# Attention of a transformer block in steps of 256 queries and four heads, with the softmax sums as products of their own

## The reference, cut to what matters

```
mod = silu(condition) @ Wada + bada            # six vectors a batch: shifts, scales, gates
xm  = layernorm(x, g1, be1) * (1 + sc_a) + sh_a
q, k, v = split(xm @ Wqkv)                     # 16 heads of 32
s   = (q @ k.T) * 32**-0.5, causal mask        # per batch and head, 1024 x 1024
x   = x + gt_a * ((softmax(s) @ v) @ Wproj + bproj)
xm  = layernorm(x, g2, be2) * (1 + sc_m) + sh_m
x   = x + gt_m * (gelu(xm @ W1 + b1) @ W2 + b2)
```

## Time and profile before

| | before |
|---|---|
| median of 3 runs | 3526.39 us |
| profiled execution | 3530.63 us |
| its span | 3528.9 us |
| mean granted TensorE clock | 0.981 |
| TensorE busy (products) | 3353.2 us, 95% |
| VectorE busy | 1776.7 us, 50% |
| ScalarE busy | 1199.3 us, 34% |
| GpSimd busy | 1025.6 us, 29% |

### The profile page before, as it was taken

One profiled execution on the slowest core, in us unless ns is written; L12 is line 12 of the kernel. 1 busy time (PEld: TensorE's weight loads), 2 busy tenths in 40 slices (PEclk: granted clock), 3 DMA queues, 4 the chain that ended last, 5 costly groups with the idle time before them and its releaser, 6 DMA issues.

```text
span 3528.9 us, 59322 instructions
## 1 busy us (share of the span) xinstructions
PE 3353.2 (95%) x19052; PEld 2422.8 (69%) x19052; DVE 1776.7 (50%) x2288; ACT 1199.3 (34%) x2578; POOL 1025.6 (29%) x1267
## 2 busy tenths in 40 slices
PE   7889999999999999998857999999999999999999
PEld 4645555555555555543327989998998998899898
DVE  4455665665666655655615444444444444444442
ACT  2135555455555455545531111111211111121111
POOL 3222232222222222222225323333332333333232
PEclk9989999999999999999988999999999999999999
DMA  5445555455555555554443222222122222212220
GB/s 205 157 135 163 161 160 173 149 166 159 164 156 166 166 154 161 161 165 142 130 107 93 71 59 65 57 56 71 51 67 60 65 57 56 71 51 71 56 60 13
DMA packets 227209, 392.77 MB, mean 111 GB/s; under 512 B 30160, under 2 KB 96720, under 8 KB 227080
## 3 DMA queue, kind: packets, MB, share of 16 engines
q1 hardware_dynamic: 213648, 369.42, 36.3%
q10 hardware_dynamic: 13440, 22.03, 1.8%
HBM read 271.71 MB, written 119.11 MB: 111 GB/s over the span
## 4 chain that ended last, share of the span: by engine, by line
PE 90%; DVE 4%; ACT 2%; issue 2%; DMA 1%; POOL 0%; SPq 0%; ACTq 0%; DVEq 0%; POOLq 0%
PE psH L740 21%; PE psY L753 20%; PE psA L652 15%; PE psA L595 10%; PE psT L629 8%; PE psP L719 5%; PE psA L591 5%; PE psS L609 4%; DVE mx L1043 2%; ACT e L822 2%; DVE psS L1039 1%; PE psP L729 1%; PE psT L555 1%; PE psA L629 1%; ACT xm_full L800 1%
## 5 line engine op out<-in xcount | busy, mean ns | idle before, releaser
L822 ACT ACTIVATE e<-psT 128x512 f32<-128x512 f32 (+3 forms) x1440 | 635.7, 491 | 671.0 <-PE psT L629 664.2
L1275 POOL TENSOR_TENSOR h_l<-h_full,h_h 128x256 fp32r<-128x256 f32 x512 | 488.6, 954 | 1122.1 <-DVE h_h L1201 1122.1
L1043 DVE TENSOR_REDUCE mx<-psS 128x4 f32<-128x2048 f32 (+3 forms) x384 | 666.4, 1757 | 211.1 <-PE psS L609 205.5
L922 ACT ACTIVATE h_full<-psH,b1c 128x256 f32<-128x256 f32 x512 | 244.0, 477 | 1333.1 <-PE psH L740 1333.1
L1201 DVE CAST h_h<-h_full 128x256 fp32r<-128x256 f32 x512 | 151.0, 295 | 899.5 <-ACT h_full L922 899.4
L740 PE MATMUL psH<-a_h,w1p_h 128*128 128x256 f32 x2048 | 578.3, 282 | 7.5 <-DVE a_l L1196 7.5
L652 PE MATMUL psA<-e,vst 128*33 128x512 f32 (+3 forms) x3072 | 578.2, 498 | 5.2 <-ACT o_sb L830 3.6
L740 PE MATMUL psH<-a_h,w1p_l 128*128 128x256 f32 x2048 | 580.7, 284 | 0.0
L740 PE MATMUL psH<-a_l,w1p_h 128*128 128x256 f32 x2048 | 580.3, 283 | 0.0
L1301 POOL TENSOR_SCALAR_AFFINE_SELECT e<-e 128x256 f32<-128x256 f32 x512 | 217.4, 426 | 927.6 <-ACT e L822 926.5
L629 PE MATMUL psT<-qst,kst 97*128 97x512 f32 (+3 forms) x1440 | 442.0, 377 | 31.7 <-ACT e L822 30.6
(11 more groups left out here) (101 smaller groups left out, 4035.5 us busy)
## 6 DMA issues: line engine op xcount, KB each, us to landing
qk_split<-qk_hl SPq DMA_DIRECT2D x128, 512.0 KB, 3.6
kst<-qk_split SPq DMA_DIRECT2D x128, 256.0 KB, 4.0
qst<-qk_split SPq DMA_DIRECT2D x128, 256.0 KB, 4.3
values<-vaug ACTq DMA_DIRECT2D x64, 264.0 KB, 2.1
vst<-values SPq DMA_DIRECT2D x32, 528.0 KB, 4.1
attended<-o_sb SPq DMA_DIRECT2D x256, 66.0 KB
xin<-in_x_dram SPq DMA_DIRECT2D x64, 256.0 KB, 4.8
kmx<-qk_split SPq DMA_DIRECT2D x32, 512.0 KB, 4.3
```

The lines of the kernel that those rows point to most:

```text
L822: act.activation(e[:, s % ERING, hd, 0:w], score_bank(s, hd, with_a)[:, 0:w], ACT.Exp, scale=SCALE)\
L922: act.activation(h_full[:, m % 4, :], psH[:, m % 4, 0:RA], ACT.Gelu, bias=b1c[:, m:m + 1])\
L1043: reduce = dve.tensor_reduce(mx[:, part, :, qt], psS[:, :, col:col + w], AX_X, ALU.max)
L1275: return pool.tensor_tensor(dst, full, high.bitcast(F32), ALU.subtract)
```

## The change

A step is now one chunk of keys by up to 256 queries for all four heads. The chunks run through quarters of the queries, the last quarter first; an item has 20 steps, a body 40, and two steps are a slot. A score bank holds two heads. Each head's values stand on output rows 32 x head, without the column of ones. The sums are separate products of `ones` (128 x 32) with exponentials, into the second half of `psO`: in the 4 slots of an item that hold the diagonal, with both chunks; in the other 6, with `es`, the sum of the slot's two tiles, which GpSimd adds. `psO` is copied after each quarter. q and k are loaded by quarters of the rows, for four heads in one transfer of 1 KB rows; the first quarter of k has two places. The sums come out 32 times over, one row of each head is stored to `s_dram`, and each MLP block loads them broadcast and inverts them on VectorE in four pieces, two blocks ahead; those of blocks 0 and 1 are inverted before the MLP starts. The normalised block goes back into `xin`, so its next load waits for the transposes. The step numbers of all other work are moved to fit 40 steps.

```diff
-NCH = 12
-IT_STEPS = 24
-BODY_STEPS = 48
+NCH = 20
+SLOTS = NCH // 2
+BODY_STEPS = 2 * NCH
+BODY_SLOTS = 2 * SLOTS
 ERING = 8
+SRING = 2
-A_SHARES = ((6, 0, 6), (2, 8, 2), (5, 1, 5, 1)) * 4
+A_SHARES = ((6, 0, 6), (2, 8, 2), (8, 4)) * 4
-TURN_AT = (40, 41, 42, 43)
-SPLIT_HI_AT, SPLIT_LO_AT = 44, 45
+TURN_AT = (34, 35, 36, 37)
+SPLIT_HI_AT, SPLIT_LO_AT = 38, 39
-LN_STATS_AT, LN_AGGR_AT, LN_NORM_AT = (20, 22, 24, 26), 28, (32, 34, 36, 38)
-MAX_AT = {1: (1, 3), 3: (1, 4), 5: (1, 5), 7: (1, 6), 9: (1, 7), 11: (1, 8)} | {15: (2, 0), 19: (2, 1), 23: (2, 2)}
+LN_STATS_AT, LN_AGGR_AT, LN_NORM_AT = (14, 16, 18, 20), 22, (26, 28, 30, 32)
+MAX_AT = {1: (1, 3), 3: (1, 4), 5: (1, 5), 7: (1, 6), 9: (1, 7), 11: (1, 8)} | {15: (2, 0), 17: (2, 1), 19: (2, 2)}
-O_COPY_AT = {6: (0, 0), 2: (1, 1)}
+O_COPY_AT = {10: (0, 0), 16: (0, 1), 0: (1, 2), 2: (1, 3)}
+LOAD_QK_AT = {8: 3, 14: 2, 18: 1}
+LOAD_K0_AT, LOAD_Q0_AT = 2, 0
+INVERT_AT = {5: 0, 9: 1, 14: 2, 15: 3}
...
+                b, hg = group(u, ahead)
+                src = src[:, :, :, bass.ds(b * T + QUART * p, QUART)]
+                sp.dma_start(tile[0:2 * HD, :, cols].bitcast(F32), src.rearrange("j c s r -> (c s) j r"))\
+                  .then_inc(done[p], 16)
...
+                bank = score_bank(s, hp, with_a)
+                for d in range(2):
+                    hd = 2 * hp + d
+                    mm = pe.matmul(bank[:, d, 0:w], kst[0:97, hd, key_cols(kt, h)], qst[0:97, q0 // HALF, hd, q0 % HALF:q0 % HALF + w],
+                                   start=True, stop=True, skip_group_check=True)
+                mm.then_inc(sem("scores_ready"), 1)
+
+            def added_sums(u, t):
+                h, i = divmod(t, SLOTS)
+                n = (u * 2 + h) * len(ADDED_SLOTS) + ADDED_SLOTS.index(i)
+                pe.wait_ge(sem("added"), n + 1)
+                past(pe, "pe")
+                for hd in range(GH):
+                    mm = pe.matmul(psO[HD * hd:HD * (hd + 1), QUART:2 * QUART], ones[:],
+                                   es[:, ADDED_SLOTS.index(i) % SRING, hd, :], start=False, stop=True,
+                                   skip_group_check=True)
+                mm.then_inc(sem("summed"), 1)
...
                 for d in range(2):
-                    half, kt, q0, w = CHUNKS[c + d]
-                    for hd in range(2):
-                        j = 2 * (pair % 2) + hd
-                        cols = slice(q0 - HALF * half, q0 - HALF * half + w)
-                        mm = pe.matmul(psO[64 * hd:64 * hd + VW, cols], vst[:, pair // 2, kt, VW * j:VW * (j + 1)],
-                                       e[:, (s + d) % ERING, hd, 0:w], start=(kt == 0), stop=True,
+                    quarter, kt, q0, w = CHUNKS[2 * i + d]
+                    c = q0 - QUART * quarter
+                    for hd in range(GH):
+                        mm = pe.matmul(psO[HD * hd:HD * (hd + 1), c:c + w], vst[:, h, kt, HD * hd:HD * (hd + 1)],
+                                       e[:, (2 * t + d) % ERING, hd, 0:w], start=(kt == 0), stop=True,
                                        skip_group_check=True)
-                    mm.then_inc(sem("pv_done"), 1)
+                if i in DIAG_SLOTS:
+                    for d in range(2):
+                        quarter, kt, q0, w = CHUNKS[2 * i + d]
+                        c = QUART + q0 - QUART * quarter
+                        for hd in range(GH):
+                            mm = pe.matmul(psO[HD * hd:HD * (hd + 1), c:c + w], ones[:],
+                                           e[:, (2 * t + d) % ERING, hd, 0:w], start=False, stop=True,
+                                           skip_group_check=True)
+                mm.then_inc(sem("pv_done"), 1)
...
                     if s % 2 == 1 and not (isinstance(u, int) and u == 0 and s == 1):
-                        values(u, s - 3)
+                        t = s // 2
+                        if t >= 2 and (t - 2) % SLOTS in ADDED_SLOTS:
+                            added_sums(u, t - 2)
+                        values(u, t - 1)
...
-            dve.wait_ge(sem("sums_loaded"), 16)
-            dve.reciprocal(x1[:, 1], x1[:, 0]).then_inc(sem("sums_inverted"), 1)
+            def invert(u, k):
+                dve.wait_ge(sem("o_loaded"), 5 * 16 * (u + 1))
+                dve.reciprocal(oin[:, 1, k], oin[:, 1, k]).then_inc(sem("sums_inverted"), 1)
...
+            for k in range(KT):
+                invert(0, k)
             for m in range(FT):
                 prepare_step(0, 0, m)
+                if m == BASE_AT:
+                    for k in range(KT):
+                        invert(1, k)
...
+            def add(u, t):
+                h, i = divmod(t, SLOTS)
+                if i in ADDED_SLOTS:
+                    n = ADDED_SLOTS.index(i)
+                    pool.wait_ge(sem("exp_done"), (u * BODY_STEPS + 2 * t + 2) * 2)
+                    wait(pool, sem("summed"), (u * 2 + h) * len(ADDED_SLOTS) + n - SRING + 1)
+                    past(pool, "pool")
+                    pool.tensor_tensor(es[:, n % SRING], e[:, 2 * t % ERING], e[:, (2 * t + 1) % ERING], ALU.add)\
+                        .then_inc(sem("added"), 1)
```

More of the change, by code:

```diff
@@ L77, in score_chunks @@
     out = []
[L78 to L81, removed]
+    for quarter in reversed(range(4)):
+        for kt in range(2 * quarter + 2):
+            q0 = max(QUART * quarter, P * kt)
+            out.append((quarter, kt, q0, QUART * (quarter + 1) - q0))
     return out
@@ L108 @@
 DIAG = [c for c, (_, kt, q0, _) in enumerate(CHUNKS) if q0 == P * kt]
-assert len(CHUNKS) == NCH
+DIAG_SLOTS = [i for i in range(SLOTS) if 2 * i in DIAG]
+ADDED_SLOTS = [i for i in range(SLOTS) if i not in DIAG_SLOTS]
+LAST_SLOT = {CHUNKS[2 * i][0]: i for i in DIAG_SLOTS}
+assert len(CHUNKS) == NCH and len(ADDED_SLOTS) % SRING == 0
 assert sorted((qt, part) for chunks, _ in MAXES for qt, part, _, _ in chunks) == \
@@ L261, in build @@
         mlp.close()
-        qk_loaded = [sem(f"qk_loaded{s}") for s in range(2)]
+        q_loaded = [sem(f"q_loaded{p}") for p in range(4)]
+        k_loaded = [sem(f"k_loaded{p}") for p in range(4)]
         m_loaded = [sem(f"m_loaded{s}") for s in range(2)]
@@ L315, in load_x @@
                 if r == 0:
-                    wait(sp, sem("xn_ready"), ia)
+                    if isinstance(ia, int) and ia <= AHEAD + 1:
+                        wait(sp, sem("xn_ready"), ia)
+                    else:
+                        sp.wait_ge(sem("a_formed"), (ia - 1) * A_N + A_TURNS)
                     past(sp, "sp")
@@ L411, in _ @@
             load_max(0, 0)
-            load_qk(0, 0)
+            load_k(0, 0, 0)
+            load_q(0, 0, 3)
+            for p in (1, 2, 3):
+                load_k(0, 0, p)
+            for p in (2, 1):
+                load_q(0, 0, p)
             load_max(0, 1)
@@ new lines, in values @@
+            def values(u, t):
+                if t < 0:
+                    u, t = u - 1, t + BODY_SLOTS
+                h, i = divmod(t, SLOTS)
+                it = u * 2 + h
+                if i == 0:
+                    pe.wait_ge(v_loaded[h], (u + 1) * 16)
+                if CHUNKS[2 * i][1] == 0:
+                    wait(pe, sem("o_copied"), it * 4 + 3 - CHUNKS[2 * i][0])
+                if i in DIAG_SLOTS:
+                    pe.wait_ge(sem("masked"), it * len(DIAG) + 2 * DIAG_SLOTS.index(i) + 2)
@@ L659, in body @@
                 for s in range(BODY_STEPS):
-                    h, r = divmod(s, IT_STEPS)
-                    for hd in range(2):
-                        scores(u, s, hd, with_a)
+                    h, r = divmod(s, NCH)
+                    for hp in range(2):
+                        scores(u, s, hp, with_a)
                     if with_ln and s in TURN_AT:
@@ L854, in body @@
                 for s in range(BODY_STEPS):
[L855 to L856 removed]
+                    h, r = divmod(s, NCH)
                     exps(u, s, with_a)
[L858 to L861 removed]
+                    if r in O_COPY_AT:
+                        back, n = O_COPY_AT[r]
+                        if not (isinstance(u, int) and u == 0 and h < back):
+                            o_copy(u, h - back, n)
                     if with_a and item_ended(s - 1) is not None and item_ended(s - 1) < A_NV:
@@ L1048, in max_join @@
                 dve.wait_ge(sem("max_reduced"), i * NMX + NMX)
-                dve.tensor_tensor(mxc[:], mx[:, 0], mx[:, 1], ALU.max).then_inc(sem("max_joined"), 1)
+                first, second = (mx[:, part].rearrange("p h (s t) -> p s h t", s=2) for part in range(2))
+                dve.tensor_tensor(mxc[:], first, second, ALU.max).then_inc(sem("max_joined"), 1)
             def max_row(u, ahead):
@@ L1313, in body @@
                     mask(u, s)
+                    if s % 2 == 1:
+                        add(u, s // 2)
                     if with_ln and s == SPLIT_LO_AT:
```

277 lines of the change are left out of this document (130 added, 147 removed).

## The result

| | before | after |
|---|---|---|
| median of 8 runs | 3528.89 us | 3542.51 us |
| lowest, highest | 3525.66, 3532.33 us | 3538.59, 3551.08 us |
| profiled execution, its span | 3530.63, 3528.9 us | 3540.59, 3538.9 us |
| mean granted TensorE clock | 0.981 | 0.967 |

The ratio is 1.0043 [1.0032, 1.0055]: the changed kernel is 0.4% slower. The forecast was 1.4% faster. The number lies inside the range and the sign is wrong.

What follows compares the result with a forecast made beforehand. TensorE's stream was taken to bound 13 of 16 bodies. From 3530.6 us, terms of -73, +43, -27, -5 and +12 made -50, so 3480.6 us, or 3476 us for the timed median; range 3405 to 3560 us.

Steps and rivals of the forecast that it cites:

- the clock's term: At the new body ends, falls of TensorE's granted clock to half were set at 1 us a body, 12 us.
- the change of stage: Between attention and MLP: 12 us off ahead of the first product, 6 back before the residual; 5 us gained (0 to 12).
- Values and sums: TensorE's attention products: four heads on four column tiles take 14.2 us an item, 2.8 less, -73 us over 13 bodies.
- The rival with 1.5 us an item: Short 128-column passes on four tiles can't start within 0.05 us of each other: 48 us more, 3524 us; chance 0.08.
- GpSimd's adds: Six adds an item on GpSimd, at 3 us each, come in time for TensorE and cost nothing.
- The end of a body: TensorE waits 3.6 us for xm_l behind a third VectorE reduction, once in each of 12 bodies: 43 us lost.
- The clock rival: The clock falls at each body end, costing 82 us instead of 12: 3546 us, slower; chance 0.17.
- The last three bodies: Attention without projection: 38.5 us an item, a gain of 4.5 in each of 6 items, 27 us (0 to 40).
- The MLP: Each block gains 4 x 1.64 us of VectorE work, with hidden tiles cast three steps ahead: no change in time.
- The rival without a body-end wait and at full clock: No wait comes up at the body end and the clock stays: -43 and -12, 3421 us; chance 0.20.

Runs made afterwards that it cites:

- kernel with both edits: The changed kernel with TensorE's two loops over bodies written out and the transposes, split and normalising two steps earlier: 3456.04 us, 0.9792 of before.

## Why the prediction was wrong, by its steps

The step that failed by most is the clock's term: 12 us were set down, and the runs put it near 40. Behind it stands a term that the sum lacks, the return of TensorE's loop, 37 us of holes in the middle bodies. With the stream's gain 10 us too good and the change of stage of the wrong sign, the span became 10 us longer where 50 us less were forecast.

The distances and starts of the two traces divide the 10.0 us by which the span grew: start +1.7, bodies with projection +29.1, last bodies -23.5, change of stage +3.4, MLP -0.7. The forecast had -3 for the first (one item), -15 for the second (25 items at -2.8, +43, +12), -27, -5 and nothing. The second is where it failed. There the terms as measured are about -59 for the products, +39.5 for holes and `xm_l`, +9 for other short waits (30.9 us before, 40.2 after) and some +40 for the clock, which makes +30.

- **Values and sums: right, a little too good.** The kernel with both edits has few other losses, so it is the best place to read this: its bodies with projection take 48.2 us less than before over 25 items. The clock cost 10 us of that (below), and other short waits are equal within 1 us, so the products are worth about 59 us where 25 x 2.8 = 70 was forecast, 2.4 us an item. Eight passes of 256 columns take 0.45 us (408.56 to 409.01), four every 0.22, for 0.21 forecast. The rule of the Trainium skill (TensorE: Matmul & The Clock Gate, Part 3), that four row tiles give 3.07x and three column tiles 2.38x, would have made the item dearer than before by an estimated 1.1 us; the stream of four column tiles here shows no such loss.
- **Can TensorE be fed: yes.** In the group of 16 passes from 409.01 us the last eight, of 128 columns, take 0.22 us, 0.027 us each, and the four of a set start 0.007 us after one another. The rival with 1.5 us an item (the fourth of the list, which the prediction's sum of chances calls the fifth) needed passes at least 0.05 us apart, and is excluded.
- **GpSimd's adds: right.** 192 of them, priced at 3 us, and no wait of TensorE on `es` in the trace:

```profile
L1376 POOL TENSOR_TENSOR es<-e 128x1024 f32<-128x1024 f32 x192 | 458.1, 2386 | 511.9 <-ACT e L882 375.9 <-PE psA L673 136.0
```

- **The end of a body: the mechanism was right, and a second one that wasn't in the sum covered it.** With the loops written out the wait for `xm_l` stands where it was put, up to 2.9 us long (forecast 3.6), 22.7 us in all (forecast 43). What the sum left out is TensorE's own program. The diff doubles the products of a slot's scores and values, and the part on the change counted their columns and passes, never the instructions of a loop pass. In the waits between 240 and 1500 us the holes are 37.0 us in ten returns, and `xm_l` 2.5 us at the two crossings without one:

```profile
PE psT L662 <- issue: 37.0, 10, 5.5
...
PE psS L637 <- DVE mx L1100: 11.5, 24, 0.7
...
PE psS L644 <- DVE mxc L1107: 4.9, 12, 0.4
PE psA L619 <- DVE xm_l L1075: 2.5, 2, 1.3
```

  These 39.5 us stand where 43 were forecast, so the size of this term came out nearly right by luck, for a reason that it didn't have. The lines on `mx` and `mxc` are short waits for the maxima (4.0 us before).
- **The clock: the step that failed in size.** 12 us were set down. Over the 25 items the kernel after is at half clock for 99.0 us, in stretches of 3.4 to 10.2 us at every body end, where before it is never. What such a stretch costs is read from the kernel with both edits: its five crossings without a fall take 48.66 us and the seven with one of 3.4 us take 50.11, so 1.45 us, 0.42 for each us at half. At that rate 99 us cost about 42 us (an estimate, since 12 of the 99 us lie in the holes). The traces bear it out: over the 25 items after takes 77.2 us more than the kernel with both edits, TensorE's waits 47.9 of them, and the 29.3 left over stand beside 75 us more at half, 0.39 each. So the clock cost some 39 to 42 us (0.41 a us is used elsewhere in this text), 27 to 30 more than forecast, which is the largest part of the miss. Holes of the loop are not needed for it: with the loop written out, which is the body end as the forecast drew it, the clock is at half for 85 us, some 35 us of cost. Only with both causes gone does it fall to 23.9 us, 10 us of cost, near the 12 set down. The clock rival had this mechanism, and its condition (a fall in more than nine bodies) was met. Its number, 3546 us, is close to the 3542.51 measured, but its price of 6.8 us a fall was double the 3.4 us or so a body end here, some 40 us too much in all, and other errors, a smaller stream gain and the change of stage among them, came to about as much. So it had the mechanism, and its number is close by luck. The Trainium skill (TensorE: Matmul & The Clock Gate, HAM oscillation) says that idle gaps bring the low clock; the fall inside the hole at 412 us agrees. The kernel with both edits also has falls without a hole near 3 us, where TensorE was busy 3.22 of 4 us:

```profile
506.00:510.00 4.00, 3.22 (x48) 2.00 (x48) 3.97 (x4) 0.21 (x1) 2.76 (x3) 0.73 0.81 205
...
607.00:611.00 4.00, 3.00 (x53) 1.96 (x53) 3.97 (x5) 0.56 (x2) 3.21 (x3) 1.00 0.80 203
```

  One body on, the same place with TensorE busy 3.00 of 4 us keeps its clock. What decides between them stays open.
- **The last three bodies: right.** -23.5 us for -27, with one return of the short loop (4.2 us) among them; with both edits it is -33.
- **The change of stage: wrong sign.** 57.1 us became 60.6. The chain of waits after:

```profile
1835.79 8.84 DMA oin<-sums
1844.66 6.60 DVE oin L1181 x4
1851.28 1.24 DVE a_full L1188
...
1854.45 11.80 DMA oin<-sums
1866.31 1.63 issue
1867.94 4.92 DVE oin L1181 x3
```

  The four first reciprocals are the 6.6 us forecast, but the broadcast loads ahead of them are 8.84 and 11.80 us in the chain. TensorE waits 17.05 us for `xc` instead of 8.51: the second four cost 8 us, forecast 6, and the 12 us off ahead of the first product were about 5 (its wait 31.64 before, 26.37 after).
- **The MLP: right.** 1648 us as before, with VectorE busy 905 us for 709 and idle 225 us in front of the reciprocals for their loads, of which nothing reaches TensorE.

With the loop's return and the `xm_l` wait taken out, the kernel stands at 3456 us. The rival without a body-end wait and at full clock gave 3421. The 35 us between are 11 of stream, 10 of clock, 8 at the change of stage and 6 in the part before 240 us, less 6 that the last bodies did better; some 6 come from how the medians of this comparison (before ran at 3529.6) stand to the profiled run and to the 3526.4 of the forecast.

## What to carry to other kernels

When a change splits products, count the instructions of one pass of the engine's loop as well as the columns: here 546 products with their loads were kept and 962 were fetched anew at each return, for 2.5 to 5.5 us. Waits at one place hide each other: two edits that gave back 30 and 22 us alone gave 86 together; when "issue" ends TensorE's idle time just where another engine is late too, take away both before judging either. And when a loop is cut into fewer steps, distances written in steps (here two steps after the transposes for four) shrink with it and must be set again.

## What the runs showed of the hardware

- A pass of 546 products and 546 weight loads stays with TensorE between passes (one packet in 1047 us); one of 802, 962 or 1092 doesn't (802 by the one return of the short loop, 4.2 us), and TensorE stands still for 1.8 to 5.5 us at each return. Where between 546 and 802 the limit lies, and whether it counts products, instructions or bytes, wasn't tried. Straight-line code of the same length shows no standstill.
- Four column tiles of 32 run four at a time in plain fp32: eight passes of 256 columns in 0.45 us, eight of 128 in 0.22, and 2.5 to 2.6 us for the 6144 columns of two passes each that were taken away or added per item, once short waits that moved the other way are put back, 0.41 to 0.42 ns a column where two tiles took 0.85.
- The granted clock can fall for only 3.4 us, at 1.45 us each; 99 us at half clock over twelve body ends don't show in a row of slices 88 us wide.
